# Transposing the normalised rows by DMA, as fp16 halves, instead of on TensorE

## The reference, cut to what matters

```python
xn = (x - mean(x)) / sqrt(var(x) + 1e-5)               # per row; x is 8 x 1024 x 512
Q, K, V = xn @ Wq + bq, xn @ Wk + bk, xn @ Wv + bv     # 1024 columns, 16 heads of 64
scores = where(abs(i - j) <= 64, Q @ K.T, 0.0)
out = softmax(scores) @ V                              # entries outside the band count as exp(0)
s = xn @ Win + bin_                                    # 64 columns
g = sum over 16 of relu(s * W1 + b1) * W2, + b2        # per column of s
result = x + out @ Wo + bo + g @ Wout + bout
```

## Time and profile before

| | us |
|---|---|
| median of 3 runs | 1940.09 |
| lowest, highest | 1938.85, 1940.41 |
| the profiled execution's own time | 1939.03 |
| its span, first to last instruction | 1937.3 |
| TensorE busy | 1841.0 (95% of the span) |
| GpSimd busy | 1593.4 (82%) |
| VectorE busy | 1544.3 (80%) |
| ScalarE busy | 1512.2 (78%) |

### The profile page before, as it was taken

How to read it: one execution, slowest core, us unless ns; L and a number is a source line. 1 busy time by engine, 2 the same in 40 slices (tenths; PEclk the granted TensorE clock), 3 DMA queues, 4 the chain that set the end, 5 groups by cost and what they waited for, 6 DMA issues and landing times.

```text
span 1937.3 us, 41951 instructions
## 1 busy us (share of the span) xinstructions
PE 1841.0 (95%) x13699; PEld 967.3 (50%) x13699; DVE 1544.3 (80%) x4207; ACT 1512.2 (78%) x4089; POOL 1593.4 (82%) x2248
## 2 busy tenths in 40 slices
PE   7889999999999999999999999999999999999996
PEld 4444455455554455454554455545455455554453
DVE  5889888887788877888778877788777887788776
ACT  4989887787787787787787887777787787778774
POOL 3788788987888977988779987898878987888974
PEclk8999999999999999999999999999999999999998
DMA  5588557766687766787658776786757866576756
GB/s 156 136 170 175 130 117 166 173 135 119 122 189 156 140 124 120 186 158 131 136 105 196 154 135 121 140 193 137 142 105 156 187 135 128 120 164 142 139 119 136
DMA packets 745594, 280.56 MB, mean 145 GB/s; under 512 B 682505, under 2 KB 694817, under 8 KB 745377
## 3 DMA queue, kind: packets, MB, share of 16 engines
q1 hardware_dynamic: 745328, 277.87, 69.2%
q10 hardware_dynamic: 48, 0.01, 0.0%
HBM read 84.84 MB, written 25.17 MB: 57 GB/s over the span
## 4 chain that ended last, share of the span: by engine, by line
PE 41%; POOL 34%; ACT 8%; issue 7%; DVE 5%; DMA 4%; SPq 0%; POOLq 0%; DVEq 0%; ACTq 0%
PE ps L1254 22%; POOL probs L426 17%; POOL p_lo L441 13%; PE ps L1269 7%; PE ps L1304 5%; ACT probs L578 3%; PE ps L1240 3%; DMA pT_lo<-p_lo 3%; POOL acc L448 2%; POOL oT_lo L433 2%; DVE probs L938 1%; PE ps L1291 1%; PE ps L1279 1%; DVE acc L985 1%; ACT oT_hi L649 1%
## 5 line engine op out<-in xcount | busy, mean ns | idle before, releaser
L1254 PE MATMUL ps<-xT_hi,w_split 128*128 128x512 f16 x3072 | 974.7, 382 | 13.6 <-DMA w_split<-w_kept 7.9
L441 POOL TENSOR_TENSOR p_lo<-probs,p_hi 128x256 f16<-128x256 f32 x1008 | 712.7, 707 | 78.4 <-ACT p_hi L641 1.2
L426 POOL TENSOR_SCALAR probs<-probs,inv_l,neg_e 128x256 f32<-128x256 f32 x1016 | 626.8, 632 | 117.3 <-DVE neg_e L957 117.0
L578 ACT ACTIVATE probs<-probs,neg_max 128x256 f32<-128x256 f32 x1024 | 505.8, 498 | 139.3 <-DVE neg_max L945 139.3
L1254 PE MATMUL ps<-xT_lo,w_split 128*128 128x512 f16 x1536 | 585.6, 381 | 0.0
L1254 PEld LDWEIGHTS ps<-xT_hi,w_split 128*128 128x128 f16 x3072 | 301.1, 98 | 396.9 <-issue 33.3
L938 DVE CUSTOM_DVE_ANT_0 probs<-ps,mask,unit_s 128x256 f32<-128x256 f32 x1024 | 433.1, 477 | 48.7 <-PE ps L1240 29.0
L985 DVE SCALAR_TENSOR_TENSOR acc<-ps,unit_o,acc 128x512 f32<-128x512 f32 x512 | 356.4, 738 | 24.2 <-PE ps L1269 24.2
L641 ACT ACTIVATE p_hi<-probs 128x1024 f16<-128x1024 f32 x256 | 267.8, 1053 | 78.5 <-POOL probs L426 77.5
L1269 PE MATMUL ps<-wo_split,oT_hi 128*128 128x512 f16 x1024 | 305.8, 380 | 12.0 <-DVE qT_lo L1027 5.2
L433 POOL TENSOR_TENSOR oT_lo<-o_sum,oT_hi 128x512 f16<-128x512 f32 x128 | 152.6, 1192 | 116.6 <-ACT o_sum L653 116.0
(11 more groups left out here) (117 smaller groups left out, 2352.4 us busy)
## 6 DMA issues: line engine op xcount, KB each, us to landing
w_split<-w_kept SPq DMA_DIRECT2D x168, 256.0 KB, 3.1
acc<-in_L_attn_x SPq DMA_DIRECT2D x14, 1024.0 KB, 7.6
out_x<-acc SPq DMA_DIRECT2D x14, 1024.0 KB, 5.8
wo_split<-wo_kept SPq DMA_DIRECT2D x56, 256.0 KB, 2.9
w_kept<-w_split SPq DMA_DIRECT2D x24, 256.0 KB, 3.0
pT_hi<-p_hi SPq DMA_TRANSPOSE x256, 3.2
pT_lo<-p_lo SPq DMA_TRANSPOSE x256, 3.3
acc<-in_L_attn_x SPq DMA_DIRECT2D x4, 512.0 KB, 5.8
```

The source lines that it names most:

```text
L426: pool.tensor_scalar(probs[:, h, t], probs[:, h, t], inv_l[:, c:c + 1], neg_e[:, c:c + 1], ALU.mult, ALU.add).then_inc(normed, 1)
L441: pool.tensor_tensor(p_split[lo][:, h, t], probs[:, h, t], p_split[hi][:, h, t], ALU.subtract).then_inc(p_lo, 1)
L578: act.activation(probs[:, h, t], probs[:, h, t], ACT.Exp, bias=neg_max[:, c:c + 1], accum_out=row_sum[:, c:c + 1])
L1254: last = pe.matmul(dst[:], w[wp][:, i, c], xT[xp][:, c, half * LINE:half * LINE + LINE], start=(c == 0 and a == 0), stop=(c == KC - 1 and ...
```

## The change

For batches 1 to 7 the rows are no longer transposed on TensorE. ScalarE copies two normalised tiles at a time as fp16 into `x_rows[hi]` (`rows_high`), VectorE subtracts to give `x_rows[lo]` (`rows_low`), and SP issues a DMA transpose of each (`transpose_rows`), 128x1024 fp16, into `xT`. `xT` is now laid out tile by tile, so a projection reads 512 columns as four runs of 128. Four copies, four subtractions and eight DMA transposes a batch take the place of 32 TensorE transposes, eight PSUM reads by ScalarE and eight by VectorE. The first batch keeps TensorE's transposes. One output tile's product moves ahead of the second V projection in k = 0.

```diff
-        xT = [sb(f"xT_{part}", [P, KC, N], F16) for part in ("hi", "lo")]
+        xT = [sb(f"xT_{part}", [P, T, KC, P], F16) for part in ("hi", "lo")]
+        x_rows = [sb(f"x_rows_{part}", [P, T, E], F16) for part in ("hi", "lo")]
...
+            def transpose_rows(b, p, part):
+                n = PAIRS * b - 1
+                sp.wait_ge((rows_hi, rows_lo)[part], rows_of(b, p))
+                if p < 2:
+                    sp.wait_ge(v_proj, 2 * n + 1)
+                else:
+                    sp.wait_ge(qk_proj, 4 * n + 4)
+                sp.dma_start_transpose(xT[part][:, two_tiles(p)].rearrange("p t c q -> p (t c) q"),
+                                       x_rows[part][:, two_tiles(p)].rearrange("p t e -> p (t e)")) \
+                    .then_inc(rows_got[p // 2], 16)
...
+                if proj and k == 0 and b > 0:
+                    transpose_rows(b, 2, hi)
+                    transpose_rows(b, 2, lo)
+                    transpose_rows(b, 3, hi)
+                    transpose_rows(b, 3, lo)
                 if attend:
                     transpose_weights(j, 0, 0, hi)
...
                     next_weights(V_)
+                if proj and k == 7 and not last:
+                    transpose_rows(b + 1, 0, hi)
+                    transpose_rows(b + 1, 0, lo)
...
                     next_weights(Q_)
+                if proj and k == 7 and not last:
+                    transpose_rows(b + 1, 1, hi)
+                    transpose_rows(b + 1, 1, lo)
...
+            def rows_high(b, p):
+                act.wait_ge(xn_ready, T * b + 2 * p - 2)
+                if b > 1:
+                    act.wait_ge(rows_got[p // 2], 64 * (b - 1))
+                act.activation(x_rows[hi][:, two_tiles(p)], xn[:, two_tiles(p)], ACT.Copy).then_inc(rows_hi, 1)
...
                     normalise(b + 1, 3)
+                    rows_high(b + 1, 0)
                 hidden_high(1)
                 if proj:
                     value_lines(1)
                     value_means()
...
                 if ln_next and k == 7:
-                    x_high(b + 1, 2)
-                    x_high(b + 1, 3)
+                    rows_high(b + 1, 2)
...
+            def rows_low(b, p):
+                dve.wait_ge(rows_hi, rows_of(b, p))
+                if b > 1:
+                    dve.wait_ge(rows_got[p // 2], 64 * (b - 1))
+                dve.tensor_tensor(x_rows[lo][:, two_tiles(p)], xn[:, two_tiles(p)], x_rows[hi][:, two_tiles(p)],
+                                  ALU.subtract).then_inc(rows_lo, 1)
...
-                            last = pe.matmul(dst[:], w[wp][:, i, c], xT[xp][:, c, half * LINE:half * LINE + LINE],
+                            last = pe.matmul(by_tiles(dst[:]), w[wp][:, i, c], xT[xp][:, four_tiles(half), c],
...
+                    if k == 0 and b > 0:
+                        pe.wait_ge(rows_got[0], 64 * b)
                     project_qk(0)
...
+                    project_out(3)
+                if proj and k == 0 and b > 0:
+                    pe.wait_ge(rows_got[1], 64 * b)
...
-                if proj and ln_next and k == 7:
-                    pe.wait_ge(ffn_added, T * b + T)
-                    transpose_x(b + 1, 0)
-                if proj and ln_next and k == 7:
-                    outputs_added(0)
-                    transpose_x(b + 1, 1)
```

More of the change, by code:

```diff
@@ L132, in band_attention_ffn @@
         xT_done, xT_hi, xT_lo = sem("xT_done"), sem("xT_hi"), sem("xT_lo")
+        rows_hi, rows_lo, rows_got = sem("rows_hi"), sem("rows_lo"), [sem(f"rows_got_{half}") for half in range(2)]
         w_hi, w_lo = ([sem(f"w_{part}_{s}") for s in "vqk"] for part in ("hi", "lo"))
@@ L714, in step @@
                     exps(2)
-                if ffn and k == 0:
-                    x_high(b, 4)
+                if n == 0:
+                    x_high(4)
+                if ffn and k == 0 and b > 0:
+                    rows_high(b, 3)
                 if proj:
@@ L1127, in step @@
                 if ln_next and k == 7:
-                    x_low(b + 1, 0)
+                    rows_low(b + 1, 0)
                 if ffn and k == 6:
@@ L1135, in step @@
                 if ln_next and k == 7:
-                    x_low(b + 1, 1)
+                    rows_low(b + 1, 1)
                 hidden_unit(1)
@@ L1152, in step @@
                 if ln_next and k == 7:
-                    x_low(b + 1, 2)
-                    x_low(b + 1, 3)
+                    rows_low(b + 1, 2)
                 if ffn and k == 0:
```

135 lines of the change are left out of this document (61 added, 74 removed).

## The result

| | before | after |
|---|---|---|
| median of 12 runs each, us | 1938.43 | 1940.91 |
| lowest, highest | 1936.41, 1940.41 | 1938.61, 1944.74 |
| the profiled execution's own time | 1939.03 | 1940.66 |
| its span | 1937.3 | 1938.8 |

The ratio is 1.0022, with a 95% interval of 1.0014 to 1.0029. I had predicted 1930.5 on the scale of 1940.09, which is 0.9951.

A forecast was written before the change was run, and what follows sets the result against it. TensorE's order of work was taken to bound k = 7 and k = 0; 4.37 - 0.9 - 1.15 - 0.95 = 1.37 us a boundary, 9.6 for seven, gave 1930.5 us on the median's scale, range 1914 to 1943.

The forecast's parts named there:

- What goes: TensorE's transposes and a wait for x_low: k = 7 gains 1.95 us, k = 0 2.42, together 4.37 a boundary.
- (a): k = 6: ScalarE's row copy delays the values' read and the network's second part; 0.9 us lost, bounds 0 to 1.0.
- (b): k = 0: subtractions slow GpSimd in k = 7, so second scores wait for kT_lo; 1.15 us, bounds 0 to 2.3.
- (c): k = 0: the second V projection waits for the last row transpose; about 0.95 us, bounds 0.5 to 1.9.
- The rival on SP's queue: k = 7 into k = 0: four more issues delay pT_lo, weigh_values(0) waits 1.9 us; 1944; most of slower's 0.18.
- GpSimd's three extra blockings, some 3 us, fit there: k = 0 and k = 1: GpSimd, busy 24.55 and 22.73 us, has room for the subtractions' extra delay.
- Seven equal boundaries: All batch boundaries: the gain summed at one, 1.37 us, was taken seven times, 9.6 us.
- The four runs of 128 columns: Projection matmuls: reading the moving operand in four runs was priced at nothing; 2 ns each would eat the gain.
- Nothing measurable: Rival for the whole kernel: the three waits reach 4.4 us together, leaving 1940; chance 0.14.

The follow-up runs named there:

- e1: Changed kernel with k = 6's ScalarE row copy moved behind the values' high half; 1938.11 us, ratio 0.9985 to the kernel before.
- e3: Changed kernel with VectorE's row subtraction cut to 8 of 1024 columns, the low half otherwise zero; 1933.88 us, ratio 0.9967 to the kernel before.
- e9: Changed kernel with each row subtraction replaced by two one-input bn_stats and an 8-column subtraction; 1935.47 us, ratio 0.999 to the kernel before.
- e6: Changed kernel with subtraction cut to 8 columns and, in k = 7, the K load ahead of one pT_hi; 1934.09 us, ratio 0.9975.
- e5: Changed kernel without the DMA row transposes and their waits, copies and subtractions kept; 1943.65 us, ratio 1.0013 to the kernel before.
- e7: Changed kernel, complete, with copies and subtractions moved into idle slots and SP's order changed, K load sooner; 1921.14 us, ratio 0.9915.
- e8: As e7, with K's last halves in k = 0 ahead of the last p_hi and the network's line; 1917.75 us, ratio 0.9901.

## Why the prediction was wrong

I took 9.6 us off; 1.5 came on in the profiled execution, 2.5 between the medians.

- **What goes: right.** k = 7 fell by 1.95, as summed. In k = 0 the 2.42 are there too: without waits it lasts 30.20.
- **(a) ScalarE in k = 6: the wait was right, the loss per boundary too large.** TensorE waited 1.3 for it instead of 0.34, at five of the six later boundaries. I took all of the 0.9 as lost for good, since TensorE has no idle time behind it. But k = 6 as a whole lost 0.45 on average, and 0.39 by e1, half of the term. At one boundary another wait stood in its place, and at two the kernel before had waits of its own in k = 6 (1.7 for weights, 0.8 for a `pT_lo`) that are gone or smaller; why they went isn't shown. Where nothing else came up, e1 got back 0.91 to 1.08.
- **(b) The late `kT_lo` in k = 0: right.** 1.15 predicted, 1.16 measured. The eight normalisations took 6.32 (6.27 by the sum). The subtractions took 1.23 us (median of 28), near my lower bound, not 1.35. The Trainium skill, "SBUF — State Buffer", section "Who interferes with whom", says that a VectorE instruction with two SBUF inputs contends with a GpSimd instruction that reads SBUF: e3 and e9 agree, and the price here is 1.0 us of GpSimd for each subtraction of 1.23, a little less than its whole length.
- **(c) The second V projection: right at four of the six later boundaries.** I forecast 0.95 there, and it waited 0.96 to 1.11. At the other two, the boundary shown among them, it waited for nothing, because the K projection had waited 1.14 and 1.11 for its weights before. e6, where that wait is gone, shows 0.96 at the V projection of the boundary shown. I had not followed the K load in SP's queue. The rival on SP's queue counted four more issues ahead of `pT_lo` and stopped there; the K load stands behind those too. For the sum of k = 0 the two are nearly the same: 32.3 forecast, 32.4 at the boundary shown, 32.62 on average.
- **"GpSimd's three extra blockings, some 3 us, fit there": the step that failed.** I had compared its busy time in k = 0 and k = 1 with the length of the steps. But what counted was the idle time between two given instructions, the 1.28 us ahead of `oT_lo`, and two blockings in k = 0, the subtraction's and `v_lo`'s, 2.0 us together, used it up. Behind the second normalisation ScalarE's in-order row holds `kT_hi`. So k = 1 lost 1.20 at six boundaries, 7.2 us; e3 and e9 give it back.
- **Seven equal boundaries: the other step that failed.** The first has its own K load at the end of SP's row, and GpSimd is further behind there: its second normalisation ended at 259.14, 1.1 us ahead of the step, against 730.44 and 2.2 us at the boundary shown. It lost 6.4 us in k = 0 where I had 0.3 gained; 3.4 us of that are the clock. The kernel before already waited 0.68 for the K weights there. e5 shows that the load is late there without any row transposes, e3 that a row transpose is 3.7 late there without the subtractions (k = 0 37.41)., taken at the third boundary, could not show it.
- **The rest.** The four runs of 128 columns cost nothing: the matmuls start 0.21 to 0.22 us apart. `pT_lo` was not waited for at the boundary shown: it went out at 734.39, and `weigh_values(0)` started at 737.97 with no wait. At two of the other five it was waited for, by 0.33 and 0.40. So the rival's delay was there, but small at its place. The rival "Nothing measurable" had nearly the number, but not the reason: it wanted the three waits of (a) to (c) to reach 4.4, and counted as waits they come to 3.1 to 3.3.

Six boundaries were 1.06 us worse each than forecast (-0.31 against -1.37), 6.4 us; the first was 4.5 worse (+3.1 against -1.37). That is 10.9 of the 11.1 us between a span 9.6 shorter and one 1.5 longer. The rest, +1.9 in the other steps, -0.9 at the start and -0.7 at the end, nearly cancels, and I don't explain it.

Why TensorE's 23 us were not to be had by any single repair: in k = 0 four results (`kT_lo`, the first half's transposes, the K weights at some boundaries, the second half's transposes) come some 1 to 2 us late, each seen in one of the runs. Taking away one or two left k = 0 at 32.4 to 32.9 in e3, e6 and e9, and in e5 what k = 0 gained k = 1 lost. Only when all came sooner, in e7 and e8, did it fall to 30.2.

## What to carry to other kernels

When TensorE loses work before a step, list every result and every load that the step wants, each with its new time against its new want, those further back in the same DMA queue as well; the smallest margin is what is gained, and the next ones lie right behind it. Ask of an engine that stands still longer not whether its busy time fits in the step, but which idle stretch takes the delay, and what is queued behind it on the engines that wait. Work the first and the last boundary out by themselves, since their queues differ. And look for a forecast wait at every boundary before you call it absent: which of two neighbouring waits shows can change from one to the next.
